# A recurrent convolution kernel on three directions: the new value's sum made in its PSUM accumulator, convolutions in two parts, context heads on VectorE

## The reference, cut to what matters

```python
def _gru_step(x, h, wih, whh):
    gi = x @ wih.T
    gh = h @ whh.T
    ir, iz, i_n = jnp.split(gi, 3, axis=-1)
    hr, hz, h_n = jnp.split(gh, 3, axis=-1)
    r = jax.nn.sigmoid(ir + hr)
    z = jax.nn.sigmoid(iz + hz)
    n = jnp.tanh(i_n + r * h_n)
    return (1.0 - z) * n + z * h
...
def step(h, xr):                      # 32 steps, one line of 8 x 32 pixels each
    out = _gru_step(xi, h, wih, whh)
    ctx = out.reshape(b, L, c).transpose(0, 2, 1)
    h_new = jnp.tanh(_conv1d(ctx, cw, cb)).transpose(0, 2, 1).reshape(b * L, c)
    return (h_new, ctx)
...
context_map = jnp.concatenate([ctx_above, ctx_below, ctx_left, ctx_right], axis=1)
out = jnp.einsum('bchw,oc->bohw', context_map, w_comb) + b_comb[None, :, None, None]
```

## Time and profile before

| what | value |
|---|---|
| median of 3 runs | 367.69 us (367.65 to 368.1) |
| the profiled execution | 366.35 us, span 364.6 us |
| granted TensorE clock over the span | 0.994 |
| busy: TensorE, VectorE, ScalarE | 324.1, 308.2, 275.0 us |
| the loop | 62 to 324 us of the span, about |

### The profile page before, as it was taken

One profiled execution on the slowest core, in us unless ns is written; L12 is line 12 of the kernel. 1 busy time (PEld: TensorE's weight loads), 2 busy tenths in 40 slices (PEclk: granted clock), 3 DMA queues, 4 the chain that ended last, 5 costly groups with the idle time before them and its releaser, 6 DMA issues.

```text
span 364.6 us, 7973 instructions
## 1 busy us (share of the span) xinstructions
PE 324.1 (89%) x2702; PEld 261.3 (72%) x2702; DVE 308.2 (85%) x766; ACT 275.0 (75%) x573; POOL 15.8 (4%) x26
## 2 busy tenths in 40 slices
PE   0002798999999999999999999999999999999995
PEld 0002477888888888888888888888888888873442
DVE  0659989999998899999999999999899888987875
ACT  6538897888888888888888888888888888867400
POOL 1056101000000000000000000000000000000000
PEclk9999899999999999999999999999999999999999
DMA  7900000000000000000000000000000000000433
GB/s 301 375 0 1 1 2 0 2 0 0 0 0 0 0 0 0 0 0 0 0 0 0 0 0 0 0 0 0 0 0 0 0 0 0 0 0 36 174 138 115
DMA packets 4182, 10.43 MB, mean 29 GB/s; under 512 B 592, under 2 KB 720, under 8 KB 4176
## 3 DMA queue, kind: packets, MB, share of 16 engines
q1 hardware_dynamic: 4176, 10.36, 7.4%
HBM read 6.16 MB, written 4.19 MB: 28 GB/s over the span
## 4 chain that ended last, share of the span: by engine, by line
PE 85%; ACT 5%; DVE 4%; issue 2%; DMA 2%; POOL 1%; SPq 0%; ACTq 0%
PE rz_bank L690 22%; PE conv_bank L690 17%; PE rz_bank L693 11%; PE n_bank L690 11%; PE conv_bank L693 8%; PE n_bank L693 5%; DMA ctx_store<-weights_dram 2%; ACT ctx_store L342 1%; PE rz_bank L776 1%; PE n_bank L776 1%; PE rz_bank L780 1%; PE n_bank L780 1%; PE n_bank L778 1%; PE rz_bank L778 1%; DVE stats L489 1%
## 5 line engine op out<-in xcount | busy, mean ns | idle before, releaser
L690 PE MATMUL conv_bank<-ctx_store,w_parts 128*128 (+1 forms) x558 | 108.9, 275 | 1.4 <-ACT ctx_store L430 0.9
L690 PE MATMUL rz_bank<-h_parts,w_parts 128*128 128x256 f16 x372 | 76.2, 273 | 0.1
L407 ACT ACTIVATE rz<-rz_bank,descale 128x512 f32<-128x512 f32 x96 | 65.9, 686 | 7.9 <-PE rz_bank L690 2.4
L419 ACT ACTIVATE nval<-npre 128x256 f32<-128x256 f32 x93 | 38.4, 413 | 40.5 <-DVE npre L627 40.5
L693 PE MATMUL conv_bank<-ctx_store,w_parts 128*128 (+1 forms) x279 | 67.2, 275 | 0.0
L690 PEld LDWEIGHTS conv_bank<-ctx_store,w_parts 128*128 128x128 f16 x558 | 54.3, 98 | 17.2 <-ACT ctx_store L430 6.6
L615 DVE SCALAR_TENSOR_TENSOR npre<-n_bank,descale,rz 128x256 f32<-128x256 f32 x93 | 45.0, 484 | 24.5 <-ACT rz L407 24.3
L690 PE MATMUL rz_bank<-x_rows,w_parts 128*128 (+1 forms) x256 | 52.8, 274 | 2.0 <-issue 2.0
L424 ACT ACTIVATE hval<-conv_bank,biases,descale 128x256 f32<-128x256 f32 x93 | 52.0, 560 | 0.0
L693 PE MATMUL rz_bank<-h_parts,w_parts 128*128 128x256 f16 x186 | 45.7, 273 | 0.0
L690 PE MATMUL n_bank<-h_parts,w_parts 128*128 128x256 f16 x186 | 45.6, 273 | 0.0
(11 more groups left out here) (110 smaller groups left out, 499.6 us busy)
## 6 DMA issues: line engine op xcount, KB each, us to landing
x<-x_dram SPq DMA_DIRECT2D x8, 512.0 KB, 9.3
out_dram<-x_rows SPq DMA_DIRECT2D x16, 256.0 KB, 2.0
ctx_store<-weights_dram SPq DMA_DIRECT2D x3, 576.0 KB, 5.1
ctx_store<-weights_dram SPq DMA_DIRECT2D x1, 192.0 KB, 6.1
biases<-biases_dram SPq DMA_DIRECT2D x1, 2.0 KB, 11.6
```

The costliest lines, as they stand in the source:

```text
L407: nc.scalar.activation(rz[k][:].rearrange("p g c -> p (g c)"), rz_bank[k][:], ACT.Sigmoid, scale=gate_scale(k)).then_inc(sig_done[k], 1)
L690: last = nc.tensor.matmul(out, w_block(HI, k, n), parts(hi_or_lo), start=start, stop=stop and hi_or_lo == LO, skip_group_check=True)
```

## The change

Four things. First, the tile `npre` and the pass `tanh_argument` are dropped: the hidden state's products for the new value go into columns 0 to 255 of `n_bank[k]`, `reset_hidden` multiplies them there by r, in place, and the input's products (`new_products`) are then accumulated on top, so that the tanh reads the sum from PSUM (with the descale as its scale). Second, the input products are split: gates a block ahead as before (`input_gates`), new value late in its own block. Third, the convolution is split: the six matmuls that need only the context's head are issued one block after it (lag 1), three before the new value's input products and three behind them; the three that need its rest come a block later (lag 2), between the hidden gates and the hidden new value. Fourth, the context's head moves from ScalarE to VectorE, between the blend and `reset_hidden`. The number of matmuls is unchanged.

TensorE's order in a block, in words: hidden gates (6), convolution rest (3, lag 2), hidden new (3), input gates of the next (6), convolution head (3, lag 1), new value's input (3), convolution head (3, lag 1).

```diff
 (ScalarE)
             def new_value(k, s):
-                if is_first(s):
-                    act.wait_ge(n_ready[k], 1)
-                    nc.scalar.activation(nval[k][:], n_bank[k][:, 0:COLS], ACT.Tanh,
-                                         scale=gate_scale(k)).then_inc(n_done[k], 1)
-                else:
-                    act.wait_ge(npre_done[k], s)
-                    nc.scalar.activation(nval[k][:], npre[k][:], ACT.Tanh).then_inc(n_done[k], 1)
+                act.wait_ge(n_full[k], s + 1)
+                nc.scalar.activation(nval[k][:], n_bank[k][:, 0:COLS], ACT.Tanh,
+                                     scale=gate_scale(k)).then_inc(n_done[k], 1)
...
                 if exists(now[1]):
                     new_value(*now)
-                if exists(before[1], STEPS - 2) and not starting:
-                    hidden(*before)
                 if exists(nxt[1]):
                     gates(*nxt)
...
-                if exists(now[1]):
-                    context_hi(*now)
                 if exists(before[1], STEPS - 2):
-                    if starting:
-                        hidden(*before)
+                    hidden(*before)
                     hidden_hi(*before)
                 if j == DIRS - 1 and exists(t + 1):
 (VectorE)
             def reset_hidden(k, s):
                 dve.wait_ge(sig_done[k], s + 1)
-                dve.wait_ge(n_ready[k], s + 1)
-                nc.vector.scalar_tensor_tensor(npre[k][:], n_bank[k][:, COLS:2 * COLS], gate_scale(k),
-                                               rz[k][:, 0, :], ALU.mult, ALU.mult).then_inc(rh_done[k], 1)
+                dve.wait_ge(n_ready[k], s)
+                nc.vector.tensor_tensor(out=n_bank[k][:, 0:COLS], in0=n_bank[k][:, 0:COLS],
+                                        in1=rz[k][:, 0, :], op=ALU.mult).then_inc(rh_done[k], 1)
+
+            def context_hi(k, s):
+                dve.wait_ge(ctx_done[k], s + 1)
+                nc.vector.tensor_scalar(context_lines(k, s, HI), context[k][:].rearrange("p b l -> p (b l)"),
+                                        ACT_SCALE, None, ALU.mult).then_inc(ctx_hi_done[k], 1)
...
-            def tanh_argument(k, s):
-                dve.wait_ge(rh_done[k], s)
-                nc.vector.scalar_tensor_tensor(npre[k][:], n_bank[k][:, 0:COLS], gate_scale(k),
-                                               npre[k][:], ALU.mult, ALU.add).then_inc(npre_done[k], 1)
...
                     blend(*now)
+                    context_hi(*now)
                 if exists(nxt[1]) and not is_first(nxt[1]):
                     reset_hidden(*nxt)
 (TensorE)
+            def new_products(k, s):
+                first = is_first(s)
...
+                if not first:
+                    pe.wait_ge(rh_done[k], s)
+                passes(n_bank[k][:, 0:COLS], k, 2, x_parts, HI, start=first)
+                passes(n_bank[k][:, 0:COLS], k, 2, x_parts, LO, stop=True).then_inc(n_full[k], 1)
...
+            def hidden_new(k, s):
...
+                pe.wait_ge(n_done[k], s)
+                passes(n_bank[k][:, 0:COLS], k, GATES + 2, parts, HI, start=True)
+                passes(n_bank[k][:, 0:COLS], k, GATES + 2, parts, LO, stop=True) \
                     .then_inc(n_ready[k], 1)
...
+            CONV_HI = [(tap, part) for tap in range(TAPS) for part in (HI, LO)]
+
+            def convolution_hi(k, s, first, end):
+                out = conv_bank[k % 2][:, 0:COLS].rearrange("p (b l) -> p b l", b=B)
+                if first == 0:
+                    ahead(pe, s + 1, *(tap_lines(k, s, HI, tap) for tap in range(TAPS)))
+                    pe.wait_ge(ctx_hi_done[k], s + 1)
+                    if k == 2:
+                        pe.wait_ge(h_done[0], s + 1)
+                    elif not is_first(s):
+                        pe.wait_ge(h_done[1 if k == 1 else 2], s)
+                for tap, part in CONV_HI[first:end]:
+                    nc.tensor.matmul(out, w_block(part, k, 2 * GATES + tap), tap_lines(k, s, HI, tap),
+                                     start=(tap, part) == (0, HI), stop=False, skip_group_check=True)
+
+            def convolution_lo(k, s):
...
+                pe.wait_ge(ctx_lo_done[k], s + 1)
...
             def steps(t, j):
-                k, s = lagged(t, j, 2)
-                if exists(s, STEPS - 2):
-                    convolution(k, s)
-                if j == 2 and isinstance(t, int) and t == STEPS - 1:
+                now, nxt, last, before = (lagged(t, j, lag) for lag in (0, -1, 1, 2))
+                if isinstance(t, int) and (t, j) == (STEPS - 1, 2):
                     pe.wait_ge(w_lo_done, SETS)
-                    pe.wait_ge(npre_done[0], STEPS - 1)
+                    pe.wait_ge(n_done[0], STEPS)
                     pe.wait_ge(ctx_lo_done[0], STEPS)
                     for c in (0, 1):
                         chunk_part(c, 0)
-                k, s = lagged(t, j, 0)
-                if exists(s) and not is_first(s):
-                    hidden_products(k, s)
+                if exists(now[1]) and not is_first(now[1]):
+                    hidden_gates(*now)
+                if exists(before[1], STEPS - 2):
+                    convolution_lo(*before)
+                if exists(now[1]) and not is_first(now[1]):
+                    hidden_new(*now)
...
-                k, s = lagged(t, j, -1)
-                if exists(s):
-                    input_products(k, s)
+                if exists(nxt[1]):
+                    input_gates(*nxt)
+                if exists(last[1], STEPS - 2):
+                    convolution_hi(*last, 0, CONV_AHEAD)
+                if exists(now[1]):
+                    new_products(*now)
+                if exists(last[1], STEPS - 2):
+                    convolution_hi(*last, CONV_AHEAD, 2 * TAPS)
...
-            pe.wait_ge(npre_done[1], STEPS - 1)
+            pe.wait_ge(n_done[1], STEPS)
             for c in (2, 3):
                 chunk_part(c, 0)
```

More of the change, by code:

```diff
@@ L38 @@
 RING = 4
+CONV_AHEAD = 3
 COMB_SET = SETS - 1
@@ L425, in hidden @@
                                      bias=biases[:, k:k + 1], scale=conv_scale(k)).then_inc(h_done[k], 1)
[L427 to L431, removed]
             def hidden_hi(k, s):
@@ L439, in steps @@
                 now, nxt, before = lagged(t, j, 0), lagged(t, j, -1), lagged(t, j, 1)
-                starting = is_first(t)
                 if exists(now[1]):
-                    ahead(act, now[1], now[1] + 1, line(*now) * (B * PAD))
+                    ahead(act, now[1], now[1] + 1)
                     new_value(*now)
-                if exists(before[1], STEPS - 2) and not starting:
-                    hidden(*before)
                 if exists(nxt[1]):
@@ L634, in hidden_lo, with z_times_h @@
                                                ALU.subtract).then_inc(h_lo_done[k], 1)
-            def z_times_h(k):
+            def z_times_h(k, s):
+                dve.wait_ge(rh_done[k], s)
                 nc.vector.tensor_tensor(out=rz[k][:, 0, :], in0=rz[k][:, 1, :], in1=hval[k][:], op=ALU.mult)
@@ L652, in steps @@
                     context_lo(*now)
-                if exists(nxt[1]) and not is_first(nxt[1]):
-                    tanh_argument(*nxt)
                 if exists(before[1], STEPS - 2):
@@ L715, in input_products, with x_parts, h_line, hidden_gates @@
                     last.then_inc(rz_ready[k], 1)
[L716 to L721, removed]
-                passes(n_bank[k][:, 0:COLS], k, 2, x_parts, HI, start=True)
-                last = passes(n_bank[k][:, 0:COLS], k, 2, x_parts, LO, stop=first)
-                if first:
-                    last.then_inc(n_ready[k], 1)
-            def hidden_products(k, s):
+            def new_products(k, s):
+                first = is_first(s)
+                def x_parts(part):
+                    return x_line(k, s, part)
+                ahead(pe, s, x_parts(HI), x_parts(LO))
+                if not first:
+                    pe.wait_ge(rh_done[k], s)
+                passes(n_bank[k][:, 0:COLS], k, 2, x_parts, HI, start=first)
+                passes(n_bank[k][:, 0:COLS], k, 2, x_parts, LO, stop=True).then_inc(n_full[k], 1)
+            def h_line(k, part):
+                return h_parts[k][:, part, :]
+            def hidden_gates(k, s):
                 def parts(part):
-                    return h_parts[k][:, part, :]
+                    return h_line(k, part)
                 pe.wait_ge(h_hi_done[k], s)
@@ L738, in hidden_products, with parts @@
                 last.then_inc(rz_ready[k], 1)
-                passes(n_bank[k][:, COLS:2 * COLS], k, GATES + 2, parts, HI)
-                passes(n_bank[k][:, COLS:2 * COLS], k, GATES + 2, parts, LO, stop=True) \
+            def hidden_new(k, s):
+                def parts(part):
+                    return h_line(k, part)
+                pe.wait_ge(n_done[k], s)
+                passes(n_bank[k][:, 0:COLS], k, GATES + 2, parts, HI, start=True)
```

(28 more changed lines are left out.)

15 lines of the change are left out of this document (8 added, 7 removed).

## The result

The changed kernel takes 373.56 us (median of 4 runs, 372.02 to 373.87) against 367.67 us before (366.76 to 368.1): 1.0155 times as long, 95% interval 1.0121 to 1.0189. Forecast was 374.8. The profiled execution took 373.42 us, with a span of 371.7 us, 7.1 more than before.

A forecast was written before the change was run, and what follows sets the result against it. TensorE was taken to bound the kernel, at 8.94 us of a 8.964 us turn. Loop +5.5, tail +1.2 and start-up +0.4 sum to +7.1 us on the median of 367.69: 374.8 us, range 368.3 to 382.

The forecast's parts named there:

- TensorE bounds both kernels, and no order of the same 81 matmuls goes below a floor: Loop: TensorE is never idle for long, and the same matmuls can't take less than 8.94 us per turn.
- My slots: TensorE's matmul start-to-start times in the loop: 54 x 0.109 + 27 x 0.113 = 8.94 us of a measured 8.964.
- The column copy delays one tanh a turn, and the convolution's head stalls for it: Block with the column copy: tanh 0.49 us late, convolution head at 5.10 against slot 4.95, stall 0.15.
- the 0.21 forecast for all stalls: Loop: 0.15 before the convolution head plus 0.06 behind the reset, making the turn 9.15 us.
- The reset's stall of 0.06: Block with the column copy: next direction's reset, priced 0.484 us, lets TensorE start at 5.50 against slot 5.44.
- The shared bank as a floor of 0.08 beneath the column's stall: Direction 0's convolution waits for direction 2's hidden activation, 2.05 against slot 1.97, hidden behind the 0.15.
- The rival built on it: Loop: everything but the bank wait hides, +0.05 per turn, +1.6, ends +1.6: 370.9 us; chance 0.2.
- Tail +1.2: Last step: new value's products wait bare 1.13 us for the last sigmoid and reset; total +1.2 us.
- Start-up +0.4: Start of the steps: first tanh waits for six more matmuls, context head no longer behind image passes; +0.4 us.
- my upper bound: Start-up: +2 us if TensorE stays at its lower clock level for some 20 slots of 0.109 more.
- No slower, by what ScalarE no longer does: Rival, loop and start-up: ScalarE's missing head gives the slack back, 366.5 us; chance 0.09 faster, 0.06 breaks even.

The follow-up runs named there:

- two columns: Changed kernel with the column copy done twice each turn, the second into a buffer nobody reads: turn 10.061 us, time 402.14 us.
- a_ahead0: Changed kernel with no convolution matmul ahead of the new value's input products (0 in place of 3): turn 9.690 us, time 390.83 us.
- a_half_column: Changed kernel with each step's column copy taking only the heads, 256 of 512 columns: turn 9.070 us, time 371.26 us.
- a_ends: Changed kernel, first step's new-value products right behind its gates, six output matmuls ahead of direction 2's new value in the last step: turn 9.095, time 371.81 us.
- a_third_bank: Changed kernel with direction 2's convolution in the free half of its own new-value bank, not shared with direction 0: turn 9.094 us, time 372.10 us.
- b_dve_context: Kernel before with only the context's head moved to VectorE, behind the blend: turn 8.903 us, time 365.37 us.

## Why the prediction was right, step by step

- **TensorE bounds both kernels, and no order of the same 81 matmuls goes below a floor.** Right. The floor is 8.903 us, reached by five kernels of both orders. My slots made 8.94 of it (each read over nine matmuls, from times given to 0.01 us), and so I read 0.03 of stall a turn in the kernel before where it has 0.06. This is the term that was mis-sized most: 0.04 of the 0.06 by which the changed turn was forecast too long (9.15 against 9.093). The increase came out at 0.129 a turn in place of 0.18, 3.9 us over 30 turns in place of 5.5.
- **The column copy delays one tanh a turn, and the convolution's head stalls for it.** Right in place: the tanh is 0.51 late (0.49 forecast), half a column moved it, two columns cost all of the second. The stall is 0.17 in the timeline and 0.19 by the turns; 0.15 was forecast for it. That 0.19 lies so near the 0.21 forecast for all stalls is partly luck, since the other 0.06 do not exist.
- **The reset's stall of 0.06.** Wrong: it does not exist, since the reset takes 0.430, not 0.484. The row that I priced it by carries a pointer that the new form lacks. That it is close to the path was right (a_ahead0). By the formula of the Trainium skill for a pass that reads PSUM (VectorE: DVE Perf Modes, the TRN2 errata) an estimate is 0.39; the measured 0.430 lies between the two.
- **The shared bank as a floor of 0.08 beneath the column's stall.** The mechanism is right, the size is 0.17. The rival built on it (only the bank wait is left, +0.05 a turn) would have come out at +0.11, as a_half_column shows.
- **Tail +1.2.** Right: 1.1 of bare wait, and a_ends gets it back; all that lies behind the last column copy is 1.4 longer.
- **Start-up +0.4.** Right, like against like: 0.34 or 0.50. In the profile after it is 1.65, because TensorE's first matmuls start 0.21 us apart up to the first tanh in that execution, which a_third_bank doesn't have. That case was my upper bound (TensorE longer at the lower clock level, some 20 slots). What decides between the two forms, no run shows. The wait that I named, the first tanh behind six gate matmuls of the next direction, is real: a_ends takes it away and gets 0.5 or 1.2 back.
- **No slower, by what ScalarE no longer does.** The gain exists (b_dve_context: 0.06 a turn), but the change spends it: its order puts tanh, two blend passes and the head between new value and convolution within one block, and there is no room left for the copy.

The span of the profiled execution, 371.7 us, is the one forecast, but only because the loop was taken 1.6 us too dear and this execution has the 1.3 us of wide spacing at its start, which the profile before lacks ahead of its first tanh. That they cancel is luck. Put together like against like, the change costs 3.7 (third to last copy) + 1.4 (behind the last) + 0.3 to 0.5 (first to third), so 5.5 to 5.7 us; the median moved by 5.9 us. The forecast of 7.1 is too high by about what the loop was taken too dear. Executions of one kernel differ by 1.3 to 1.9 us, as the two forms of the start-up do; for those without a profile that this is the reason is not shown.

## What to carry to other kernels

When an engine is the bound and a change only rearranges what it waits for, write down the chain from one late instruction to the next as a sum of durations and compare it with the block: here the slack of the context's head was 0.32 us, and one copy of 1.09 us in another engine's queue, which made a tanh 0.51 late, used it up once a turn. What is lost is the lateness less the slack: 0.19 with one copy, 1.16 with two. Two waits that end within 0.02 us of each other hide one another; taking either away alone shows nothing, and only both together show the price. Before a bundle of four edits is judged, run each alone: one of these was worth 0.06 us a turn, and the bundle lost 0.13. And before two profiles are compared, compare their start-ups: two kernels with the same first step differ here by 1.3 us.

## What the runs showed of the hardware

- TensorE resumed at different distances from what released it: 0.06 us after VectorE's head (185.11 to 185.17), 0.05 after ScalarE's head before, but 0.14 after the hidden activation (183.66 to 183.80), where the wait is the second of two that stand in a row. Behind the reset in a_ahead0, where the reset's wait is the third in a row, it was 0.15, 0.15 and 0.06 in the three blocks of a turn. Why is open.
- A product in place in PSUM, 256 columns by a tile in SBUF, takes 0.430 us on VectorE; an SBUF pass of that length takes 0.42.
- A two-input VectorE pass that started 0.48 us into a GpSimd copy of 1.30 us took 1.10 in place of 0.42 us; the one that started just ahead of the copy (182.94) took 0.42.
- In the profile after, matmuls of 256 columns started 0.21 us apart from 41.87 to 44.21, the distance of the lower clock level (1.2 GHz), while the granted clock of that stretch reads 1.00. In the kernel before, too, matmuls start 0.21 apart, from 42.99 to 45.76, and there the reading is 0.50. In both TensorE had stood idle before its first matmul of the steps, 1.9 and 2.0 us; before that of a_third_bank it had so for 1.9 us too. The spacing is what counts. The rows of the two stretches, after and then before (length, busy times, clock, DMA):

```profile
41.00:44.00 3.00, 2.30 (x11) 1.66 (x12) 3.00 (x7) 1.78 (x2) 0.00 (x0) 1.00 0.01 3
...
43.00:46.00 3.00, 3.00 (x16) 2.14 (x15) 2.83 (x6) 2.87 (x7) 0.00 (x0) 0.50 0.00 0
```

And TensorE's timeline in the profile after, starts 0.21 to 0.22 us apart, then that of a_third_bank in the same place, 0.11 apart, with a granted clock of 1.00 as well:

```profile
43.79 0.42 PE L675 MATMUL rz_bank<-x_rows,w_parts 128*128 128x256 f16 x1
44.00 0.42 PE L672 MATMUL rz_bank<-x_rows,w_parts 128*128 128x256 f16 x1
44.21 0.39 PE L672 MATMUL n_bank<-x_rows,w_parts 128*128 128x256 f16 x1
44.43 0.28 PE L675 MATMUL n_bank<-x_rows,w_parts 128*128 128x256 f16 x1
```

```profile
42.91 0.27 PE L675 MATMUL rz_bank<-x_rows,w_parts 128*128 128x256 f16 x1
43.02 0.27 PE L675 MATMUL n_bank<-x_rows,w_parts 128*128 128x256 f16 x1
43.12 0.27 PE L678 MATMUL n_bank<-x_rows,w_parts 128*128 128x256 f16 x1
```
